# A GNN block on one core: in the last two layers the message loop does one node cut of the first dense matmul instead of two

## What is computed

```python
e = edge_attr @ We + be
m = jax.nn.relu(x[src] + e)
agg = jax.ops.segment_sum(m, dst, num_segments=x.shape[0])
h = ((1.0 + eps) * x + agg) @ W1 + b1
mu = jnp.mean(h, axis=0)
var = jnp.mean(jnp.square(h - mu), axis=0)
h = (h - mu) * jax.lax.rsqrt(var + BN_EPS) * gamma + beta
h = jax.nn.relu(h)
return jax.nn.relu(h @ W2 + b2)
```

## Time and profile before

| | |
|---|---|
| median of three runs | 2035.81 us (2031.61 to 2037.8) |
| the profiled execution | 2037.95 us, of it 2036.2 us span |
| mean granted clock of PE | 0.877 of full speed (2.4 GHz) |
| PE busy | 1668.8 us, 82% of the span |
| POOL, DVE, ACT busy | 1199.9, 1184.2, 852.2 us |
| chain that ended last, by engine | PE 39%, POOL 38%, issue 13%, DMA 4%, DVE 4%, ACT 2% |
| layer 2: dense stage from the first late matmul to the end of the second matmul | 1431.5 to 1479.8 us |
| layer 3: the same | 1838.2 to 1889.2 us |

### The profile page before, as it was taken

The page is one execution under the profiler, slowest core; times in us unless marked ns, Lnnn a source line. Parts: engine busy times, 40 slices in busy tenths (PEclk is TensorE's granted clock), DMA queues, the critical chain, the costliest instruction groups (busy, mean ns, idle before and its releaser), DMA issues.

```text
span 2036.2 us, 21480 instructions
## 1 busy us (share of the span) xinstructions
PE 1668.8 (82%) x7091; PEld 771.7 (38%) x7091; DVE 1184.2 (58%) x2210; ACT 852.2 (42%) x860; POOL 1199.9 (59%) x1156
## 2 busy tenths in 40 slices
PE   2877888777766668888987998999879989998695
PEld 1333333233322224344442333444423334444563
DVE  6566656572478877666434665665346656654423
ACT  1555444442034333333312655666126656661120
POOL 5777777760177778878504777774047777740032
PEclk8998888787867768887788999999889999998697
DMA  6777776761477666666316777774277777745244
GB/s 218 201 203 203 201 200 200 220 207 31 150 200 201 197 197 181 181 182 184 101 63 192 240 222 223 217 203 130 64 199 236 223 221 215 204 126 187 92 126 153
DMA packets 123184, 366.14 MB, mean 180 GB/s; under 512 B 20888, under 2 KB 25328, under 8 KB 122813
## 3 DMA queue, kind: packets, MB, share of 16 engines
q0 software_dynamic: 89840, 294.46, 50.7%
q1 hardware_dynamic: 33229, 70.23, 10.5%
HBM read 344.66 MB, written 19.95 MB: 179 GB/s over the span
## 4 chain that ended last, share of the span: by engine, by line
PE 39%; POOL 38%; issue 13%; DMA 4%; DVE 4%; ACT 2%; DVEq 0%; POOLq 0%; SPq 0%; ACTq 0%
PE ps L1452 38%; POOL ring L665 36%; DMA ring<-x_table,idxT 1%; DMA zT<-slot_table 1%; ACT ring L1296 1%; DVE ring L840 1%; POOL ring L708 1%; DMA mix<-in_edge_weight 0%; PE ps L1826 0%; DMA x_table<-ring 0%; ACT zT L1393 0%; POOL ring L717 0%; PE ps L1794 0%; DMA stage<-y_table,slot_i 0%; DVE stats L765 0%
## 5 line engine op out<-in xcount | busy, mean ns | idle before, releaser
L665 POOL DMA_INDIRECT ring<-x_table,idxT x1096 | 1153.7, 1053 | 619.1 <-issue 324.1
L840 DVE SCALAR_TENSOR_TENSOR ring<-we_bc,wT,ring 128x512 f32<-128x512 f32 x1096 | 743.2, 744 | 264.7 <-DMA ring<-x_table,idxT 264.2
L1296 ACT ACTIVATE ring<-ring 128x3072 f32<-128x3072 f32 (+1 forms) x178 | 483.7, 2718 | 604.2 <-DVE ring L840 604.2
L1452 PE MATMUL ps<-ring,onehot 128*32 128x512 f32 x2192 | 416.5, 687 | 230.7 <-ACT ring L1296 224.4
L1452 PE MATMUL ps<-ring,zT 126*128 126x512 f32 (+1 forms) x676 | 287.2, 544 | 21.8 <-DVE zT L904 21.8
L1452 PEld LDWEIGHTS ps<-fold,parts 128*128 128x128 f32 (+1 forms) x1488 | 201.8, 211 | 190.6 <-issue 182.4
L1452 PEld LDWEIGHTS ps<-ring,onehot 128*32 128x32 f32 x2192 | 77.4, 116 | 476.8 <-ACT ring L1296 267.9
L1339 ACT ACTIVATE ring<-ps 128x512 f32<-128x512 f32 x260 | 146.6, 605 | 256.9 <-PE ps L1452 256.9
L1452 PE MATMUL ps<-fold,parts 128*128 128x32 f32 (+1 forms) x1488 | 222.9, 296 | 2.8 <-ACT parts L1305 2.8
L1452 PEld LDWEIGHTS ps<-ring,zT 126*128 126x128 f32 (+1 forms) x676 | 119.2, 196 | 178.7 <-issue 166.2
L881 DVE TENSOR_TENSOR aggT<-ps,aggT 128x128 f32 x212 | 60.8, 287 | 203.7 <-PE ps L1452 200.5
(11 more groups left out here) (245 smaller groups left out, 1091.9 us busy)
## 6 DMA issues: line engine op xcount, KB each, us to landing
ring<-x_table,idxT POOLq DMA_INDIRECT x1096, 3.8
zT<-slot_table SPq DMA_DIRECT2D x26, 625.0 KB
w<-in_L_gnn_W SPq DMA_DIRECT2D x8, 1024.0 KB, 8.4
ring<-in_L_ffn_W SPq DMA_DIRECT2D x16, 512.0 KB, 9.3
x_table<-ring SPq DMA_DIRECT2D x30, 250.0 KB
x_table<-ring SPq DMA_DIRECT2D x17, 256.0 KB
y_table<-aggT SPq DMA_DIRECT2D x17, 256.0 KB, 2.0
ring<-in_x SPq DMA_DIRECT2D x1, 2304.0 KB
```

Of the source, the lines that this page charges most:

```text
L665: gp.indirect_dma_start(out=slots[:, k, u, :], out_offset=None, in_=table[:, :], in_offset=bass.IndirectOffsetOnAxis(ap=idx, axis=0)).then ...
L840: ins = v.scalar_tensor_tensor(out=slots[:, k, u, :], in0=we_bc[:, :], scalar=wT[:, c, u:u + 1], in1=slots[:, k, u, :], op0=ALU.mult, op1= ...
L1296: a.activation(at, at, ACT.Relu).then_inc(relu_done, 1)
L1452: return nc.tensor.matmul(o, lhsT, rhs, start=start, stop=stop)
```

## The change

In the last two layers only cut 0 is early. The four sums of cut 1 leave the steps 36 to 39 of the message loop, and with them their four statistics on DVE and four copies on ACT; the dense stage does them with cut 2. ACT then reads the h of cut 1 from PSUM, and the second matmul of these layers gets the wait that layer 0 has. All counters that number the early sums are adapted (`early_before`). All that the diff holds:

```diff
     def early_cuts(l):
-        return 1 if is_first(l) else 2
+        return 1 if is_first(l) or l in MIXED else 2
 
     def early_before(l):
-        return 0 if is_first(l) else l * 8 - 4
+        return sum(early_cuts(x) for x in range(l)) * KD
...
-    EARLY_MIXED = {21: 0, 24: 1, 27: 2, 30: 3, 36: 4, 37: 5, 38: 6, 39: 7}
+    EARLY_MIXED = {21: 0, 24: 1, 27: 2, 30: 3}
...
             if l not in MIXED:
                 return ps[3 + e % 2]
-            return ps[7] if e <= KD else ps[e - 1]
+            return ps[7]
...
                 pe.wait_ge(w2_loaded, l * 16 + 16)
-                if is_first(l):
-
-                    pe.wait_ge(z_ready, 2 * KD)
+                if early_cuts(l) == 1:
+
+                    pe.wait_ge(z_ready, l * 3 * KD + 2 * KD)
                 for t in range(NT):
```

## The result

| | before | after |
|---|---|---|
| median of 20 runs | 2027.65 us (2021.39 to 2044.63) | 2045.89 us (2029.64 to 2059.55) |
| ratio | | 1.007, 95% interval 1.0048 to 1.0093 |
| the profiled execution, span | 2036.2 us | 2035.1 us |

A forecast was written before the change was run, and what follows sets the result against it. PE was taken to bound the loop's end in layers 2 and 3. Layer 2: -11.2 + 15.6 + 4.9 = +9.3; layer 3: -11.2 + 14.15 + 3.65 = +6.6; together +16 us, giving 2052 us, range 2044 to 2060.

The forecast's parts named there:

- the loop, from chunk 35 to the first late matmul: Message loop end, layers 2 and 3: without the four early sums it gains 11.2 us a layer, bounds 8.7 to 14.3.
- late matmuls and scale and shift: Dense stage, first late matmul to first zT: at layer 0's 26.61 us, adds 15.6 us in layer 2, 14.15 in layer 3.
- second matmul behind its new wait: Dense stage, first zT to second matmul's end: waiting for the eighth zT adds 4.9 us in layer 2, 3.65 in layer 3.
- the walk through the steps: Layer 2, steps 36 to 39 without early sums: 2.6, 5.1, 8.7 us won at steps 36, 37, 38; 11.2 in all.
- The last step: Step 39, layer 2: flush to last group sums takes 4.15 us instead of 6.57; last sums start at 1415.85, not 1427.01.
- Moved queues: SP's next-layer edge terms and w1, and layer 3's expert weights, move with the dense stage, hidden by the second matmul's 36 us.
- the level of the forecast in microseconds: Whole kernel: profiled 2037.95 us becomes 2054; on the median of the runs, 2.1 us lower, 2052 us, 0.8% slower.
- rival 2: Loop gives only 8.7 us a layer, both layers pay layer 0's dense price, clock takes more: +26, 2062 us; chance 0.16.
- 1 (every matmul counts): PE bounds the loop to its end: 14.3 us gained a layer against 17.8 in the dense stage, 2043 us; chance 0.13.
- 3 (the gathers end the loop): Loop end follows the gathers: 16.4 us gained a layer against 17.8, 2039 us, no difference; chance 0.05.
- 4 (DVE's waits): DVE's 12.7 us of waits for early sums set the steps' pace: 27 us gained a layer against 19.3, 2020 us; chance 0.03.
- 5 (the sums filled pauses): Removed sums only filled PE's pauses, loop ends as before: +38 us for both layers, 2074 us; chance 0.03.

The follow-up runs named there:

- The second series: Kernel before and changed kernel, files unchanged, both run again on a chip where the kernel before takes 2032 us: ratios to before 0.9989 and 1.0106.
- spare matmuls: Kernel before plus matmuls with unread results in PE's short waits at each layer's loop end and between the dense matmuls of layers 1 to 3: ratio 0.9915.
- the kernel with the wait only: Kernel before, but in layers 2 and 3 the second matmul waits for eight zT instead of the first: ratio 1.0057 to before.

## Why the prediction was right and where it was off

**The direction and the mechanism** were right, by the forecast's own steps. In us for both layers, with the mean of the two profiles of each kernel on the faster chips:

| term | forecast | measured |
|---|---|---|
| the loop, from chunk 35 to the first late matmul | -22.4 | 79.6 to 57.7 = -21.9 |
| late matmuls and scale and shift | +29.8 | 23.7 to 51.2 = +27.5 |
| second matmul behind its new wait | +8.6 | 76.2 to 84.0 = +7.8 |
| sum | +16.0 | +13.4 |

The ratio of 1.007 says 14 us (10 to 19), the pieces 13.4, so they leave nothing over. The second series is less tidy: its ratio of 1.0106 says 22 us (14 to 29), its pieces 12.5. Its profiles are 6.3 us apart at the end of layer 1 already, where the kernels are the same, so scatter of this size lies outside the pieces; that all of the loss lies in them is likely, but not shown.

**Step by step.** The loop: the walk through the steps was right to 0.4 us up to chunk 38. The last step was mis-sized when PE's clock fell in its idle times, which the forecast didn't look at; it took that clock's cost only in the dense stage. The late matmuls: the term was taken as layer 0's, 26.6 us, and measured at 23.9 to 26.7, depending on where the clock fell; at full clock 23.9 against 9.6, that is 14.3 a layer. Layer 0 itself took 26.6 us in the forecast's profile only and 25.6 to 25.8 in three others, so a part of the 2.3 us by which the term was too high is the choice of one execution. The wait: forecast 42.2 us from the first `zT` to the end, measured 41.9 to 42.2, and alone it costs the same. Moved queues: the first gather of layer 3 follows the end of layer 2's second matmul after 9.5 us in both kernels, so neither the loads nor the stores cost anything there.

**What failed is the level of the forecast in microseconds**, the step that reads "on the median of the runs, 2.1 us lower, it is 2052 us". It added a difference of 16 us to a median of three runs, 2035.81. Twenty runs of that kernel have the median 2027.65 and span 23 us. So the level was 8 us too high, over half the size of the effect. The range of 2044 to 2060 us stands for ratios of 1.004 to 1.012 on the level it was made for, which holds the measured 1.007; on the level of twenty runs the same ratio gives 2042 us, below its lower end. Even the forecast's own 16 us would have come to 2044 there, the range's edge, while the measured 14 on the level of the forecast give 2050, well inside: it is the level that puts the forecast out, and the 2.6 us that the sum was too high come on top. That the median of the twenty runs after, 2045.89, lies inside the range is luck, since the medians lie 18 us apart and the ratio says 14. The chances were loose at the edges as well: most of rival 2 was counted inside, and its own figure is 2062. A range for a change as small as this one has to hold the uncertainty of the level, too, or be given as a difference.

**The rivals.** 1 (every matmul counts): the loop gains 11 us a layer and not 14.3, as ACT's relu holds PE before chunks 36 and 37 and again in step 39 (the four waits in the rows above are 3.3 us). 2 (less from the loop, more to the clock): in layer 2 of the first profile the loop did give only 8.6 us, and the clock took 3.1 us at its end and 2.2 in the late matmuls; but the three other layers of the two profiles gave 11.3 to 11.9, and the whole came out below the forecast, not 10 us above it. 3 (the gathers end the loop): its 16.4 us a layer weren't reached. 4 (DVE's waits): 1.3 of the 11 us. 5 (the sums filled pauses): put back, they cost 8.9 us a layer or more.

**Where the gain went.** The sums are equally long in both places, 14.3 us out of the loop and 14.3 into the dense stage. The loss is what the loop had hidden: about 3 us a layer in which PE now waits for ACT and DVE at the loop's end, and about 4 us because the banks of the second matmul are full of the first one's results until ACT has read them.

## What to carry to other kernels

Work that runs early on the bound engine in a loop isn't free there, but it fills the waits that appear as the loop runs out; moved behind the loop it costs its full length, and it occupies banks that the next stage needs. Price such a move by walking through the last steps of the loop with the durations of the trace, and take the dense stage from a layer that already has the new form. Where a matmul engine's short waits can't be removed, try spare matmuls into a free bank: they gave more here than the placement of the sums. And if the effect is under 1%, compare pieces that begin and end at the same instructions, and don't tie a range to the median of three runs.

## What the runs showed of the hardware

The granted clock of PE fell to half among waits of less than 2 us at the end of a loop, in one execution and not in another of the same instructions; 80 instructions of the second matmul took 36.2 to 37.6 us behind waits of 4 to 10 us, and 34.61 behind one filled with spare matmuls. The Trainium skill, page "TensorE: Matmul & The Clock Gate", section "Why this matters for your kernels", asks for no idle gaps between bursts of matmuls; these rows agree, and add that filling the gaps is worth 0.85% of this kernel (0.6 to 1.1). The forecast had used that rule only to say that nothing more could be lost, and had not asked what could be won.

The same kernel took 2032 us on one chip and 2294 and 2288 on two others. The page of the kernel with the wait only, from the one with 2294:

```profile
DMA packets 123184, 366.14 MB, mean 159 GB/s; under 512 B 20888, under 2 KB 25328, under 8 KB 122813
...
PE 47%; another core or an unknown queue 15%; DVE 14%; issue 10%; ACT 7%; POOL 3%; DMA 3%; DVEq 1%; SPq 0%; POOLq 0%; ACTq 0%
```

The mean rate is 159 GB/s instead of 180 with the same bytes, and 15% of the chain lies with something outside this core, a releaser that the kernel before doesn't show on the first chip. The group sums of chunk 36 come 17.9 us after those of chunk 35 there, instead of 10.9. What holds the gathers on these chips was not tried and stays open. The changed kernel itself didn't run on them; the pieces of its variants behind chunk 36 differ from those of the faster chips by no more than the clock explains.
